# Moving one score unit and its row maxima across the batch boundary of a hand-scheduled transformer layer

## The reference

```
q = concat(x @ Wq1, x @ Wq2)          # 2 x 16 heads of 16 channels
k, v = x @ Wk, x @ Wv                 # 16 heads, shared by both query sets
p = softmax(causal(q k^T / 4))        # 32 score matrices of 256 x 256 a batch
y = p1 @ v - sigmoid(x @ Wlam) * (p2 @ v)
x1 = layernorm(x + y @ Wo)
out = layernorm(x1 + shared_mlp(x1) + w(x1) * routed_mlp(x1))
```

## Time and profile before

| | us |
|---|---|
| median of 3 runs | 504.98 (504.73 to 506.27) |
| the profiled execution | 506.3 |
| its span, first to last instruction | 504.6 |
| TensorE busy (matmuls) | 426.5 (85%) |
| VectorE busy | 329.9 (65%) |
| ScalarE busy | 238.7 (47%) |
| GpSimd busy | 226.6 (45%) |
| mean granted TensorE clock | 0.947 of full |

### The profile page before, as it was taken

The page is one execution under the profiler, slowest core; times in us unless marked ns, Lnnn a source line. Parts: engine busy times, 40 slices in busy tenths (PEclk is TensorE's granted clock), DMA queues, the critical chain, the costliest instruction groups (busy, mean ns, idle before and its releaser), DMA issues. The chain is left out here.

```text
span 504.6 us, 10452 instructions
## 1 busy us (share of the span) xinstructions
PE 426.5 (85%) x4008; PEld 340.2 (67%) x4008; DVE 329.9 (65%) x882; ACT 238.7 (47%) x532; POOL 226.6 (45%) x283
## 2 busy tenths in 40 slices
PE   5106596799999999989899999999999998997994
PEld 5105334676688758976698568865887678766984
DVE  3503614873478586886787677857786769776685
ACT  4600384237535672548434843576255831582240
POOL 8200465426526572447334743656254731373041
PEclk9755979879999999999999999999999999999999
DMA  8793498128703690249212950378024910000000
GB/s 299 165 124 49 117 132 173 32 84 115 99 2 99 92 133 27 68 90 136 58 38 83 126 105 11 107 92 121 22 76 74 136 46 0 5 2 22 1 23 21
DMA packets 34371, 40.43 MB, mean 80 GB/s; under 512 B 3856, under 2 KB 27920, under 8 KB 34064
## 3 DMA queue, kind: packets, MB, share of 16 engines
q1 hardware_dynamic: 34320, 39.75, 43.3%
HBM read 27.94 MB, written 11.53 MB: 78 GB/s over the span
## 5 line engine op out<-in xcount | busy, mean ns | idle before, releaser
L998 DVE TENSOR_REDUCE neg_max<-ring 128x2 f32<-128x512 f32 (+3 forms) x176 | 105.8, 635 | 40.2 <-PE ring L689 38.3
L473 ACT ACTIVATE prob<-ring 128x512 f32<-128x512 f32 x192 | 100.7, 612 | 14.7 <-PE ring L710 14.5
L374 POOL TENSOR_TENSOR h_lo<-h_full,h_hi 128x256 fp32r<-128x256 f32 x72 | 53.0, 736 | 108.0 <-ACT h_hi L433 108.0
L384 POOL TENSOR_SCALAR_AFFINE_SELECT prob<-prob 128x512 f32<-128x512 f32 x128 | 83.9, 679 | 32.7 <-ACT prob L473 32.7
L626 PE MATMUL ff<-x1T_hi,wg_lo 128*128 128x256 f32 x288 | 85.7, 298 | 1.2 <-DVE h_full L1014 1.2
L628 PE MATMUL ff<-x1T_hi,wg_hi 128*128 128x256 f32 x288 | 80.3, 279 | 0.0
L627 PE MATMUL ff<-x1T_lo,wg_hi 128*128 128x256 f32 x288 | 80.3, 279 | 0.0
L684 PE MATMUL ring<-mask_b,ident_b 128*128 128x128 bf16 (+2 forms) x176 | 46.0, 262 | 32.4 <-DMA k_stack<-qk_parts_dram 27.2
L481 ACT ACTIVATE gate_t<-ff 128x256 f32<-128x256 f32 x72 | 27.6, 384 | 76.5 <-PE ff L628 73.7
L689 PE MATMUL ring<-k_stack,q_stack 96*128 96x256 bf16 (+3 forms) x512 | 61.2, 241 | 0.0
L738 PE MATMUL ybank<-prob,v_ones 128*32 128x256 f32 (+1 forms) x1024 | 55.7, 335 | 3.3 <-issue 2.0
(11 more groups left out here) (166 smaller groups left out, 954.8 us busy)
## 6 DMA issues: line engine op xcount, KB each, us to landing
q_stack<-qk_parts_dram SPq DMA_DIRECT2D x48, 256.0 KB, 9.5
qk_parts_dram<-parts SPq DMA_DIRECT2D x72, 128.0 KB
k_stack<-qk_parts_dram SPq DMA_DIRECT2D x8, 384.0 KB, 14.8
xt_raw<-xT SPq DMA_DIRECT2D x8, 256.0 KB, 2.8
k_stack<-qk_parts_dram SPq DMA_DIRECT2D x8, 256.0 KB, 11.7
xz<-x SPq DMA_DIRECT2D x8, 256.0 KB, 3.6
out<-xz SPq DMA_DIRECT2D x7, 256.0 KB, 2.2
prob<-w_gu SPq DMA_DIRECT2D x1, 1152.0 KB, 7.0
```

The lines of the kernel that those rows point to most:

```text
L374: pool.tensor_tensor(h_lo[:, n, :], h_full[:, n % RING, :], h_hi[:, n, :].bitcast(F32), ALU.subtract).then_inc(h_lo_done, 1)
L384: pool.affine_select(out=v, in_=v, compare_op=ALU.is_ge, fill=0.0, base=0, pattern=[[0, 2], [HALF, 2], [0, 2], [1, HALF]], channel_multipl ...
L473: act.activation(prob[:, g % RING, u, :], ring[u][:, :], ACT.Exp, scale=SCALE).then_inc(exp_done, 1)
L998: dve.tensor_reduce(neg_max[:, columns.start:columns.stop, i], ring[u % RING][:, 0:len(columns) * keys].rearrange("p (h k) -> p h k", k=keys),
```

## The change

The first score unit of batch i+1 with its wait for the stacks, and its maxima, go from the start of iteration i+1 to the end of iteration i: on TensorE behind the second V job and in front of the output projection, on VectorE behind `yT_second` and in front of `add_input`. Iteration 0 keeps its own first unit. From the second batch on the loop over the maxima then begins with unit 1, and norm step n follows the maxima of unit n+1.

```diff
--- before.py
+++ after.py
@@ -852,12 +852,18 @@
                     mm = down(bank, t, range(SHARED_UNITS, FF_UNITS), SHARED_UNITS, FF_UNITS - 1)
                 mm.then_inc(routed_full, 1)
 
+            def first_scores(b):
+                pe.wait_ge(stack_loaded, (b + 1) * (16 * STACK_LOADS))
+                s_unit(b, 0)
+
             def iteration(i, has_next, has_prev, has_last):
                 if i == 2:
                     pe.wait_ge(mlp_w_lo_done, W_DOWN)
-                pe.wait_ge(stack_loaded, (i + 1) * (16 * STACK_LOADS))
+                if not has_prev:
+                    first_scores(i)
                 for u in range(S_UNITS):
-                    s_unit(i, u)
+                    if u > 0:
+                        s_unit(i, u)
                     if has_next and u in QK_AT:
                         qk_job(i + 1, QK_AT.index(u))
                     if has_last and u in SHARED_AT:
@@ -894,6 +900,7 @@
                 yT_job(i)
                 if has_next:
                     v_job(i + 1, 1)
+                    first_scores(i + 1)
                 wo_job(i)
 
             for n in range(QK_JOBS):
@@ -1141,12 +1148,14 @@
                 norm2 = stepper(norm2_step, (i - 2) * LN_STEPS)
                 if has_prev:
                     before = stepper(attn_step, i * ATTN_STEPS - NORM1_STEPS + TT)
-                for u in range(S_UNITS):
+                if not has_prev:
+                    row_max(i, 0)
+                for u in range(1, S_UNITS):
                     row_max(i, u)
                     if has_prev:
 
-                        if u < NEWTON + 4:
-                            first_norm_step(u, *before)
+                        if u < NEWTON + 5:
+                            first_norm_step(u - 1, *before)
                         if u - 2 == X1T_AT:
                             x1T_second(i - 1)
                         if u - 1 == LOGIT_AT:
@@ -1180,6 +1189,8 @@
                 if has_prev:
                     mlp_unit(i - 1, FF_Y1)
                 yT_second(i)
+                if i + 1 < B:
+                    row_max(i + 1, 0)
                 add_input(i)
                 norm_stats(0, xz[i % X_SLOTS], *attn)
```

## The result

The changed kernel takes 506.75 us (median of 20 runs, 504.46 to 508.37); the kernel before took 504.8 beside it (20 runs). The ratio is 1.0038, interval 1.0021 to 1.0054: slower by about 2 us, small but outside the interval.

A forecast was written before the change was run, and what follows sets the result against it. TensorE's chain of work (busy 85%) was taken to set the time. Batches 2 to 6 +2.65, batch 1 +0.05 and batch 7 -0.35 sum to +2.35 us on the median of 504.98: 507.3, range 502.2 to 508.8.

The forecast's parts named there:

- Unit 0 in the gap: TensorE before the output projection: unit 0 fits the 0.70 us idle, so everything behind the projection's start comes 0.46 earlier.
- Maxima 0 free of cost: VectorE behind yT's low half: maxima 0 take 0.61 us of idle time, and add_input stays at 307.46.
- Step 5 starting 0.08 behind GpSimd: VectorE, batches 2 to 6: step 5's L969 is blocked until GpSimd ends, delaying maxima 7; unit 10 loses 0.53 us.
- the term of 2.65: Batches 2 to 6: each 0.53 us longer, five times, +2.65 us in all.
- The named wait: TensorE before unit 10, batches 2 to 6: a new wait for maxima of about 1.0 us.
- Batch 7: Last batch, without Q/K jobs: ScalarE's normalizing starts earlier, x1T near 424.27 against 424.62, -0.35 us.
- Batch 1: Batch already limited by VectorE: step 5 is held, unit 10 comes at 100.6 against 100.55, +0.05 us.
- the second (the step slips past): Rival, batches 2 to 6: L969 at +0.08 slips past GpSimd; -2.4 us, 502.6; chance 22%.
- The first (all is gained): Rival: 0.46 us gained at each of seven boundaries, 501.8; chance 5%.
- The third (the clock behind the boundary of batch 1 stays up): Rival, batch 1: shorter idle keeps TensorE's clock up, worth an estimated 1.6 us; +0.75, 505.7; chance 8%.
- Stacks were never late: Rival: stacks come late in front of the projection, each us costing one us a boundary; chance 2%.
- the new gap of 0.82: Rival: the new gap before unit 10, forecast as 1.0 us, lowers the clock in every batch; 510 and up; chance 3%.

The follow-up runs named there:

- e1: Changed kernel with norm step n again behind maxima n, as before; unit 0 and its maxima stay moved: 500.62 us, ratio 0.9945.
- e4: Changed kernel with all seven norm steps as early as their inputs allow, 4 to 6 behind maxima 3: 499.74 us, ratio 0.9930.
- e5: Changed kernel with norm steps 5 and 6 put behind maxima 7: 501.78 us, ratio 0.9944.
- e7: Changed kernel with GpSimd's subtractions L359 and L365 cut to 16 of 512 columns behind the first batch, output wrong: 496.36 us, ratio 0.9846.
- e9: Changed kernel with norm steps as early as possible in batch 1 and step n behind maxima n in batches 2 to 7: 499.16 us, ratio 0.9904.
- e11: Changed kernel, step n behind maxima n in batches 2 to 7; batch 1 early, but steps 5 and 6 behind maxima 6: 497.46 us, ratio 0.9872.
- e10: Changed kernel with an extra unused 128x256 ScalarE copy that makes GpSimd's second L359 start later: 500.70 us, ratio 0.9930.
- e8: Kernel before, unit 0 not moved, with the seven norm steps as early as their inputs allow: 502.01 us, ratio 0.9952.
- e6: Kernel before with GpSimd's subtractions L359 and L365 cut to 16 of 512 columns in batches 1 to 7, output wrong: 498.92 us, ratio 0.9899.
- e2: Kernel before with only the norm steps shifted, step n behind maxima n+1; unit 0 and its maxima not moved: 508.86 us, ratio 1.0120.
- e12: Changed kernel with an extra unused 128x16 ScalarE copy, which made GpSimd's second L359 0.1 us later: 501.08 us, ratio 0.9937.
- e3: Kernel before with unit 0 moved on TensorE alone; VectorE keeps its old order of maxima and norm steps: 502.71 us, ratio 0.9985.

## Why the prediction came out right

The forecast was 507.3 and the measurement 506.75, slower as predicted, and by the mechanism it named. By its steps:

- Unit 0 in the gap. It did as counted: 0.46 predicted, 0.45 seen from projection to unit 1, and again at unit 10 of batch 5 (12.35 or 12.36 behind `yT_lo` for 12.81) in e1, e4, e5, e7, e9 and e11. Over whole batches less is left: 0.38 in e1, 0.40 in e10, 0.30 in e4 against e8, 0.24 in e7 against e6. What takes it back behind unit 10 stays open, and the prediction, which let the whole batch follow unit 10, had no term for it.
- Maxima 0 free of cost, `add_input` unmoved behind the projection's end: so, 306.07 is 2.45 behind `yT_lo`, exactly as 307.46 behind 305.01.
- Step 5 starting 0.08 behind GpSimd: 0.07 to 0.14 in the five batches, held until GpSimd's end in each, then maxima 7, then unit 10 after 0.60. For unit 10 +0.53 was predicted, and it came +0.54 (13.35 behind `yT_lo` for 12.81); the five batches came out +0.59 on average (+2.95 for the term of 2.65). In batches 2 to 4 it is 0.50 to 0.54, in 5 and 6 0.59 and 0.81; the excess of those two is of the size of the scatter and was not pursued.
- The named wait was to be about 1.0 and is 0.82, while the delay is 0.99: unit 10 stands 13.35 behind `yT_lo` and 12.36 in e1. The rows of matmuls overlap (at the end of batch 0 the mask matmul at 83.67 lasts 0.39 and the next starts at 83.90), so idle time counts from a modelled end that is later than the place of the next start. I took a delay for an idle time. The cost over whole batches is 0.97 each (after against e1) and 1.03 (e2 against before).
- Batch 7: -0.35 predicted, -0.33 measured, but by another way, so that the close agreement is luck. ScalarE's normalizing was to start 0.13 earlier; it starts 9.98 behind `yT_lo`, where it was 9.92 behind. TensorE came to the x1T job earlier, at 424.07, and waited inside it, 0.84 for 0.60. The result, `x1T_hi`, is 11.60 behind `yT_lo` (424.95 - 413.35) for 11.92 before (425.26 - 413.34).

```profile
423.33 1.09 ACT L503 ACTIVATE xz<-xz,ln_shift,ln_t 128x256 f32<-128x256 f32 x2 [9.36 <-DVE ln_shift L990]
424.95 0.60 ACT L433 ACTIVATE x1T_hi<-misc 128x512 fp32r<-128x512 f32 x1 [0.53 <-PE misc L781]
```

- Batch 1: +0.05 predicted, -1.05 in the one profile. The waits came back as counted (step 5's pair of L974, at 96.98, is held for 0.78), and unit 10 stands 13.17 behind `yT_lo` for 13.34:

```profile
86.11 0.55 PE L626 MATMUL ybank<-wo_hi,yT_lo 128*128 128x256 f32 x1 [1.82 <-ACT yT_hi L433]
...
97.13 0.23 PE L684 MATMUL ring<-mask_b,ident_b 128*128 128x128 bf16 x1 [1.43 <-DVE neg_max L1005]
98.49 0.23 PE L684 MATMUL ring<-mask_b,ident_b 128*128 128x128 bf16 x1 [0.96 <-DVE neg_max L1005]
```

The other 0.9 comes behind unit 10, where the clock was 0.62 and then 1.00 for 0.50 and 0.69 (from 100 to 104, from 104 to 108). The windows are fixed and the execution stood 1.9 earlier, so this is only argued. Whether it is the change or the scatter of this batch stays open; e1 and e2 show 55.14 and 55.68.

The sum of the profile's terms is 2.95 - 1.05 - 0.33 = +1.6, and behind the last `yT_lo` the execution after is 0.3 shorter (504.0 - 463.62 for 504.6 - 463.94), which makes +1.3; the measurement is +1.95, the forecast +2.35. The five batches carry the result by the mechanism as predicted. That the whole number came so near owes something to scatter, since batch 1 was off by 1.1 in the one profile.

Of the rivals, the second (the step slips past) was the near one, and the runs show how near: e12 moves GpSimd by 0.1 us and turns +1.95 into -2.8. That -2.8 is close to the rival's -2.4. Its other condition, that a start as close as 0.08 behind is let through, is refuted by ten batches out of ten (after and e2). The first (all is gained) needs another order of the steps; that is e1. The third (the clock behind the boundary of batch 1 stays up) didn't happen: it is still down there (0.74 from 84 to 88 and 0.83 from 88 to 92, for 1.00 and 0.68 before, whose execution stood 1.9 later). The runs showed a larger prize at another place in that batch, the second fall, from 100 to 104, and VectorE's order wins it. Stacks were never late, and the new gap of 0.82 didn't bring the clock down (1.00 from 301 to 321 in the changed kernel's windows).

The page "Advanced Engine Details and Errata" of the Trainium skill, VectorE Performance Modes, was quoted for both directions of blocking. Its note speaks of VectorE instructions in a mode that it calls 2p; whether L976 runs in one, no run here shows, so that note does not by itself say that this instruction is held. The direction that mattered agrees: VectorE is held. Of the other there is only a trace: where the step starts 0.01 ahead of GpSimd or with it (two batches of e12, five of e4, three of e8), GpSimd's instruction lasts 1.19 or 1.20 instead of 1.16. It didn't let the step through in the changed kernel.

## What to carry to other kernels

When work is moved into a gap of the busiest engine, follow the second engine's order to the first place where it hands over late, here maxima 7, seven units on: the gap was free, but the shift by one that came along wasn't, and the two are separate edits. Where two engines can hold each other, read start times to a hundredth; a place that clears by 0.1 us is not cleared, and the order should be chosen so that nothing critical stands behind the instruction that may be held. A profile whose start scatters by more than the effect is read by differences within it, batch by batch, and not by its span.

## What the runs showed of the hardware

- A hold by GpSimd goes by who starts first, to about 0.01 us. Up to GpSimd's start VectorE's 128x2 instruction takes its 0.15 or 0.16 (e12, e4). At 0.01 behind both are seen (e8: 0.16 in batch 3, 1.17 in batch 5). From 0.03 behind on it lasts until 0.01 to 0.03 past GpSimd's end, up to 1.15. The first instruction of a pair (128x1) that was in flight when GpSimd started took its usual time, and the second, 0.05 behind GpSimd's start, was held (together the 1.26 of e3).
- VectorE's busy time includes the hold: +4.4 us with the same 882 instructions.
- An extra copy of 128x16 on a third engine, ScalarE, made the kernel about 5 us faster (+1.95 against the kernel before became -2.8) by delaying GpSimd 0.1 us in five batches.
- In batch 1 TensorE's waits for maxima up to unit 10 add up to 2.9 to 4.0 us in the eight profiles where its clock was down from 100 to 104, and to 0.3 to 2.5 in the six where it was up. In e4 and e9 TensorE also works little from 92 to 96 (2.24 and 2.10 of 4 us), and the granted clock from 96 to 104 is 1.00 all the same. What decides it these runs don't say.
- The start of the kernel scatters from profile to profile: the first `yT_lo` lies between 83.0 and 87.2 us. In the ten profiles where what it waits for is unchanged (all but e6, e7, e10 and e12, whose edits begin earlier) it is 84.0 to 87.2.
